# Third layer: averaging the normalised x with the probabilities in two float32r parts, and folded value weights

## What is computed

```python
xn = _layernorm(x, axis=-1)
x = x + _L2_attn_ref(xn, Wq, Wk, Wv) + _L2_ffn_ref(xn, ...)

def _L2_attn_ref(x, Wq, Wk, Wv):           # H, R = 8, 64; d = 128
    Q = (x @ Wq.T).reshape(b, n, H, R)
    K = (x @ Wk.T).reshape(b, n, H, R)
    V = (x @ Wv.T).reshape(b, n, H, d)     # 1024 columns
    attn = softmax(einsum('bnhr,bmhr->bhnm', Q, K), axis=-1)
    return einsum('bhnm,bmhd->bnd', attn, V)      # summed over the heads

def _L2_ffn_ref(x, ...):                   # ternary weights, D_HID = 512
    h = silu(tlin(x, w1)) * tlin(x, w2)
    h = gelu(tlin(h, h1)); h = gelu(tlin(h, h2))
    return tlin(h, w3)
```

## Time and profile before

| | before |
|---|---|
| median of 3 runs (us) | 1756.85 |
| the profiled execution, its time (us) | 1757.49 |
| its span, first to last instruction (us) | 1755.6 |
| mean granted clock of TensorE | 0.975 |
| PE / DVE / ACT / POOL busy (us) | 1668.1 / 996.3 / 837.4 / 406.9 |

### The profile page before, as it was taken

One profiled execution on the slowest core, in us unless ns is written; L12 is line 12 of the kernel. 1 busy time (PEld: TensorE's weight loads), 2 busy tenths in 40 slices (PEclk: granted clock), 3 DMA queues, 4 the chain that ended last, 5 costly groups with the idle time before them and its releaser, 6 DMA issues. The chain is left out here.

```text
span 1755.6 us, 22810 instructions
## 1 busy us (share of the span) xinstructions
PE 1668.1 (95%) x8686; PEld 1004.2 (57%) x8686; DVE 996.3 (57%) x1649; ACT 837.4 (48%) x1048; POOL 406.9 (23%) x331
## 2 busy tenths in 40 slices
PE   7799999999889999999999999999999997999997
PEld 4232222223555667878778786877778673444443
DVE  4555555543675454444555454454555447888886
ACT  5667777776435533333334343343344343444442
POOL 1000000000553322030211112030211205655563
PEclk8799999999889999999999999999999998999999
DMA  2222222222007610000000000000000001000000
GB/s 81 52 49 49 49 49 49 49 49 111 17 26 190 150 27 1 2 0 2 1 1 1 1 1 1 1 1 1 1 1 1 1 1 51 7 7 7 6 13 12
DMA packets 20553, 49.10 MB, mean 28 GB/s; under 512 B 1184, under 2 KB 2080, under 8 KB 19680
## 3 DMA queue, kind: packets, MB, share of 16 engines
q1 hardware_dynamic: 20448, 47.66, 11.1%
HBM read 45.17 MB, written 2.36 MB: 27 GB/s over the span
## 5 line engine op out<-in xcount | busy, mean ns | idle before, releaser
L524 ACT ACTIVATE probs<-ps 128x1024 f32<-128x1024 f32 x256 | 245.9, 1024 | 88.7 <-PE ps L780 85.8
L1972 PEld LDWEIGHTS ps_o<-v,probs 128*128 128x128 f32 x2048 | 236.8, 192 | 35.2 <-issue 30.1
L1972 PE MATMUL ps_o<-v,probs 128*128 128x129 f32 x2048 | 248.2, 278 | 1.7 <-ACT probs L1656 1.2
L1656 ACT ACTIVATE probs<-ps_ring 128x1024 f32<-128x1024 f32 x128 | 127.0, 1023 | 201.9 <-PE ps_ring L1953 201.6
L1748 DVE TENSOR_REDUCE negmax<-ps_o 128x2 f32<-128x1024 f32 x64 | 78.5, 1226 | 137.0 <-PE ps_o L1928 137.0
L794 PE MATMUL ps<-probs,v 128*32 128x512 f32 x1024 | 136.7, 607 | 0.9 <-DVE o_sb L601 0.9
L1649 ACT ACTIVATE xn<-ps_ring,pack 128x512 f32<-128x512 f32 x64 | 40.6, 685 | 164.0 <-PE ps_ring L1493 164.0
L2174 POOL TENSOR_TENSOR rs<-r,state 128x512 f32<-128x512 f32 x64 | 86.2, 1349 | 91.6 <-DVE state L2340 91.6
L1761 DVE RECIPROCAL rden<-ps_o 128x2 f32<-128x2 f32 x128 | 21.5, 168 | 147.8 <-PE ps_o L1972 147.8
L2340 DVE TENSOR_TENSOR_SCAN state<-decay,state,kv 128x511 f32<-128x511 f32 x64 | 99.1, 1548 | 6.9 <-issue 1.5
L780 PEld LDWEIGHTS ps<-q_stack,k_stack 32*128 32x128 f32 x512 | 31.4, 185 | 123.3 <-issue 96.1
(11 more groups left out here) (418 smaller groups left out, 3431.3 us busy)
## 6 DMA issues: line engine op xcount, KB each, us to landing
cwb<-combine_by_expert SPq DMA_DIRECT2D x8, 2048.0 KB
score<-score_by_expert SPq DMA_DIRECT2D x15, 1024.0 KB, 8.0
pack<-pack_dram SPq DMA_DIRECT2D x1, 3840.0 KB, 15.2
x<-x_in SPq DMA_DIRECT2D x2, 1024.0 KB, 6.1
out<-x SPq DMA_DIRECT2D x8, 256.0 KB, 2.0
pack<-pack_dram SPq DMA_DIRECT2D x1, 1992.0 KB, 8.1
pack<-pack_dram SPq DMA_DIRECT2D x1, 1543.0 KB, 6.4
pack<-pack_dram SPq DMA_DIRECT2D x1, 1140.0 KB, 9.4
```

The source lines that it names most:

```text
L524: nc.scalar.activation(probs[n % 3][:, 2 * half:2 * half + 2, :], ps, ACT.Exp, scale=float(HD0) ** -0.5).then_inc(read, 1)
L1656: nc.scalar.activation(probs[:, n % 2, m, :, :], ps, ACT.Exp).then_inc(read, 1)
L1972: last = nc.tensor.matmul(ps_o[:, i, k * (D + 1):(k + 1) * (D + 1)], probs[:, (b * PAIRS + p) % 2, m, j, queries], v[:, m, h, :], start=(m ...
```

## The change

- `values`, `take_v` and `v` go. So does `times_v`.
- `turn_x` turns the normalised x of a batch (four 128x128 transposes); ScalarE and VectorE take it as `xt_high` and `xt_low` [tokens, 128]. Column 0 of it is set to one: since the normalised x sums to zero over the features, feature 0 can be written by the others, and its place carries the ones for the softmax's sum. `fold` is Wv.T with row 0 subtracted from all rows (`fold_first`, once: two float32 matmuls), and a 129th column that picks feature 0.
- `exponent` writes to `exped` (three buffers), then ScalarE makes a second pass, `probs_high`, and GpSimd subtracts to `probs_low`.
- `mix` (b, p, m): 6 float32r matmuls of 512 columns accumulate, over the four key tiles m, the averages of x for both heads in `ps_o`. ScalarE copies them to SBUF (`take_mixed`), and `project_mixed` (4 float32 matmuls of 129 columns for a head) applies `fold`. `normalise` reads that from the ring.
- The low parts of q and k of pairs 2 and 3 are made by GpSimd from a second ScalarE copy, no longer by VectorE.
- `project_mixed` of pair 3 and `turn_attention` run in the next batch; `low_x`, `square`, `rstd`, the mean and variance of the next batch's norm move in the loop.
- Wv moves from the pack of weights that is split in two parts to the pack that is loaded whole; pieces of the split shrink from 480 to 416 columns (L1336, L1352).

```diff
 def ring_order2():
-        for t in range(FT):
-            order += [("gate", b, t), ("qk"[t % 2], b, t // 2), ("v", b, t)]
+        for t in range(FT):
+            order += [("gate", b, t), ("qk"[t % 2], b, t // 2)]
+        order.append(("turn_x", b))
+        if b:
+            order += [("out", b - 1, PAIRS - 1, 0), ("out", b - 1, PAIRS - 1, 1)]
+        order.append(("h1", b, 0))
...
@@ gpsimd
+                for n, name in enumerate("qk"):
+                    was_read(pool, (name, b, 1))
+                    nc.gpsimd.tensor_tensor(single(low[name][:, 2:4, :]), exped[:, n, :, :], high[name][:, 2:4, :], ALU.subtract
+                                            ).then_inc(low_ready, 1)
...
+                for p in range(PAIRS):
+                    for m in range(NBLK):
+                        n = tile_of(b, p, m)
+                        pool.wait_ge(high_ready, b * HIGHS2 + 5 + p * NBLK + m + 1)
+                        nc.gpsimd.tensor_tensor(single(probs_low[:, m, :, :]), exped[:, n % EXPED2, :, :], probs_high[:, m, :, :],
+                                                ALU.subtract).then_inc(low_ready, 1)
+                if b + 1 < B:
+                    low_x(b + 1)
@@ scalar
             def take_high(b, name, i):
...
+                if i:
+                    if b:
+                        act.wait_ge(low_ready, b * LOWS2)
+                    nc.scalar.activation(exped[:, "qk".index(name), :, :], ps, ACT.Copy).then_inc(read, 1)
+            def turned_high(b):
+                ps, _ = filled(act, ("turn_x", b))
+                nc.scalar.activation(single(xt_high[:, :, 1:D]), ..., ACT.Copy).then_inc(high_ready, 1)
+            def take_mixed(b, p):
+                act.wait_ge(values_done, tile_of(b, p, NBLK - 1) + 1)
...
+                nc.scalar.activation(mixed, ps_o[:, :, :], ACT.Copy).then_inc(top_read, 1)
             def exponent(b, p, m):
...
-                nc.scalar.activation(probs[:, n % 2, m, :, :], ps, ACT.Exp).then_inc(read, 1)
+                nc.scalar.activation(exped[:, n % EXPED2, :, :], ps, ACT.Exp).then_inc(read, 1)
+                was_read(act, ("score", b, p, m))
+                if n >= NBLK:
+                    act.wait_ge(values_done, n - NBLK + 1)
+                nc.scalar.activation(single(probs_high[:, m, :, :]), exped[:, n % EXPED2, :, :], ACT.Copy).then_inc(high_ready, 1)
@@ vector
+            def turned_low(b):
+                dve.wait_ge(high_ready, b * HIGHS2 + 5)
+                ps, read = filled(dve, ("turn_x", b))
+                nc.vector.tensor_tensor(single(xt_low[:, :, 1:D]), ..., xt_high[:, :, 1:D], ALU.subtract).then_inc(read, 1)
@@ tensor
+            def mix(b, p, m):
...
+                pe.wait_ge(low_ready, low_count(b, p, m))
+                for n, (lhsT, rhs) in enumerate(((xt_low, probs_high), (xt_high, probs_high), (xt_high, probs_low))):
+                    for j in range(2):
+                        last = nc.tensor.matmul(ps_o[:, j, :], single(lhsT[:, m, :]), single(rhs[:, m, j, :]),
+                                                start=(m == 0 and n == 0), stop=(m == NBLK - 1 and n == 2))
+                last.then_inc(values_done, 1)
+            def project_mixed(b, p, j):
+                ps, done = empty(pe, ("out", b, p, j))
...
+                for m in range(NBLK):
+                    first = (m % 2) * (D + 1)
+                    last = nc.tensor.matmul(ps[:, m // 2, first:first + D + 1], mixed[:, j, m * P:(m + 1) * P], fold[:, 2 * p + j, :],
+                                            start=True, stop=True)
...
                 for p in range(PAIRS):
-                    for s in range(HALVES):
-                        times_v(b, p, s)
...
+                    for m in range(NBLK):
+                        mix(b, p, m)
+                        if p + 1 < PAIRS:
+                            scores(b, p + 1, m)
+                        if p + 2 < PAIRS and m < 2:
+                            maxima(b, p + 2, 2 * m)
+                            maxima(b, p + 2, 2 * m + 1)
+                        if p + 2 < PAIRS and m == 2:
+                            turn_max(b, p + 2)
+                        if p and m in (1, 2):
+                            project_mixed(b, p - 1, m - 1)
```

270 lines of the change are left out of this document (145 added, 125 removed).

## The result

| | before | after |
|---|---|---|
| median of the runs (us) | 1758.09 (4 runs) | 1773.91 (4 runs, 1769.92 to 1776.99) |
| ratio after / before | | 1.0078, 95% interval 1.0057 to 1.0099 |
| the profiled execution, its time and span (us) | 1757.49, 1755.6 | 1771.17, 1769.4 |
| third layer, first gate to the end of the last turned attention (us) | 817.0 | 830.8 |
| of it batch 0 / each of batches 1 to 6 / last batch (us) | 101.7 / 99.7 / 116.9 | 97.3 / 100.8 / 128.8 |

The change makes the kernel slower by 0.8%: 15.8 us between the medians, 13.7 us between the profiled executions. The forecast was 1777. In the profiles the whole difference lies in the third layer (+13.8). A span alone is a coarse measure here: the third layer begins at 633 to 645 us in the profiles of this study, though the code ahead of it is the same apart from the split of the weights.

A forecast was written before the change was run, and what follows sets the result against it. TensorE, busy 95% of the span, was taken as the bound, so its saved work counts less every new wait. Batches 1 to 7 +16.8, batch 0 +1.6, ends +4.0 - 2.4: +20.0 on 1757.49, forecast 1777 us, range 1741 to 1796.

The forecast's parts named there:

- projections, batches 1 to 7: From first gate to `hide1`: walking the chain of hand-offs starts `hide1` at 16.0 instead of 17.24 us, 1.2 us gained.
- feed-forward: Stretch after the projections: the four transposes of the attention, moved here, cost 0.4 us a batch.
- loop, waits: Loop: 1.3 us for the DMA, 0.85 at pair 1's first `project_mixed`, 0.1 for `take_mixed`, less 0.2 before: +2.05.
- loop, TensorE's own work: Loop matmuls: `mix` 22.1, `project_mixed` 5.4, switches 5.0 added; `times_v` 28.6 and its interruptions 2.8 removed: +1.1 us.
- batch 0 in all, with the clock at its start: Batch 0: `hide1` 1.6 us earlier, loop +3.2, and -2.4 from a faster clock at the start; -0.8 in all.
- last batch beyond the others: End of the layer: the tail behind the last `mix` takes 6.4 us instead of 2.5, said +4.0.
- third layer: Whole change: +16.8 us for batches 1 to 7, +1.6 for batch 0, ends +4.0 - 2.4; total +20.0.
- Rival A: Third layer: hand-offs hide and TensorE's own work decides; batch 97.4 us, kernel 1739 us, faster. Chance 0.20.
- B: Projections and loop: the waits (about 38 us in all) are half as long; 1758 us, no change. Chance 0.12.
- C: Projections: idle time drops TensorE's clock in each batch for 12 matmuls, +17 us; 1794 us. Chance 0.08.
- the filled hole: Layer start: `fold_first` fills TensorE's 3.83 us idle time, so 12 matmuls may step 0.23 us: -2.4, or nothing.
- Rival D: Loop: VectorE holds up GpSimd, a tile takes 3.5 us, loop 56 instead of 50.6; 1820 us. Chance 0.04.

The follow-up runs named there:

- e1_table: Changed kernel with ScalarE's table for tanh and GELU loaded ahead of a batch's last `take_mixed` instead of behind it; ratio to before 1.0036, projections 15.02 instead of 15.98 us.
- e8_turn_before: Changed kernel with the maxima of pair 1 turned ahead of the last scores of pair 0 instead of behind them; ratio to before 1.0060, batch 99.9 against 100.8 us.
- e9_split: Changed kernel with the third product of `mix` between scores and maxima in four tiles, four more row-count changes and back a loop; loop 50.64 to 50.70 us against 49.4.
- e5_light: Changed kernel with GpSimd making the low part of only 8 of 512 probability columns in the last batch; last batch 120.8 us against 128.8, one run.
- e6_two_spreads: Changed kernel with two spread buffers for the fourth layer's norm, VectorE centring the next group before scaling the last; ratio to before 1.0032, last batch 119.8 us against 128.8.
- four edits: Changed kernel with earlier table load, `turn_x` before the last k, pair 1's maxima turned earlier, two spread buffers; 1750.79 us, ratio to before 0.9952.
- e10_two_products: Changed kernel without `mix`'s third product (high x times low probabilities); loop 43.1 to 43.2 us in five of the first seven batches against 49.4, one run.

## Why the prediction was right, and where its terms were not

| step | predicted | measured |
|---|---|---|
| projections, batches 1 to 7 | -1.2 (`hide1` at 16.0) | -1.26 (15.98) |
| feed-forward | +0.4 | +0.31 |
| loop, waits | +2.05 | +1.83 (1.94 idle, 0.11 before) |
| loop, TensorE's own work | +1.1 | +0.25 |
| batch 0 in all, with the clock at its start | -0.8 | -4.45 |
| last batch beyond the others | +4.0 | +10.8 |
| third layer | +20.0 | +13.8 |

**What held.** That the loop's work does not fall, and that new hand-offs come on top, was right in sign and nearly in size. The walk of the projections gave each point within 0.1 us: tanh 2.54, the end of the turned low part, `hide1`. The chain was what it said: e1_table took 0.95 out of one link, and 0.96 came back at the end. The DMA's wait was 1.23 where 1.3 was taken, and e8_turn_before showed its cause; ScalarE's second pass took 1.060 (1.058 taken). Rival A (the hand-offs hide) is excluded by the 15.98 and the 1.23; B would have needed waits half as long. C's clock did fall, but not in the projections, where no wait is over 0.65: it fell in the last batch, where no rival had put it.

**The mis-sized term: what the interruptions of `times_v` had cost before.** The loop came out at +2.08 instead of +3.2; 0.85 of the difference is TensorE's own work, 0.2 the waits. The prediction priced the same thing in two ways: 0.42 for each of the 12 changes and back after, from two maxima inside `hide1`, but about 0.3 for each of the 9 interruptions before, 2.8 in all. For those it had counted the longer steps of the 16 records and of the first pair of the scores, and not that of the last pair, 0.32 instead of 0.23. The traces give the same 0.39 to 0.40 on both sides: 9 x 0.39 = 3.5 before, 12 x 0.39 = 4.7 after (5.0 taken). So 0.7 us too little was taken off for before and 0.3 too much added for after; 96 matmuls of `mix` at a step of 0.2325 instead of 0.23 give 0.2 back. That turns +1.1 into +0.3. The rule that the prediction took from the Trainium skill, TensorEngine Tiling (Array Packing), Key Properties, says that changing the tiling mode drains TensorE. The trace agrees in so far as each change costs time in both directions, and e9_split gives the price; but the rule counts against the kernel before, with its 9 interruptions, three quarters as much as against the one after.

**Batch 0 was walked wrongly.** `hide1` was put at 15.2; it started 12.91 after the first gate, with the releaser of gate 3 (`xn` L1799). Without the two `project_mixed` of a batch before, the ring place of `hide1` is that of gate 3: it is three ring uses behind gate 3, not behind `turn_x`, so nothing of the tail is on its path. The clock's part was right: 19.21 before against the 16.8 of the walk is the 2.4 us predicted for the filled hole, and the granted clock at 636 to 640 is 1.00 after.

**The last batch held what no rival had in the right place.** Rival D expected VectorE to hold up GpSimd, tile by tile. It is the other way: in the kernel after GpSimd's subtractions keep to 2.36 to 2.43 us whatever VectorE does, and VectorE's multiplications with two operands in SBUF wait for them, up to 2.8 instead of 0.68 us. The Trainium skill, SBUF — State Buffer, "SBUF: two separate sides", says that an instruction with two SBUF inputs contends with a GpSimd instruction that reads SBUF, and that the one that starts first keeps the ports for its whole length. The traces agree: in the kernel after GpSimd was first each time that a multiplication was longer, and where VectorE was first, in e6_two_spreads, its multiplication took 0.69 and the subtraction 2.57. They also agree in that an instruction with one operand in PSUM is not held up: the turned low part takes 0.69 all eight times (L1776) while GpSimd is at a subtraction. In batches 0 to 6 the one such instruction had slack. In batch 7 there are seven, five of them held up by 1 us or more in a chain that TensorE waits for, and two of these waits were long enough that the clock fell behind them. The tail behind the last `mix` is 4.2 of the +10.8, where 4.0 was predicted, and 6.6 are left for the hold-up. e5_light and e6_two_spreads show cause and remedy; they give back 8.0 and 9.0, more than the 6.6. So without the hold-up, and apart from its tail, the change would cost this batch 1.4 to 2.4 us less than it costs the others; why was not followed.

**The sum.** The errors have opposite signs: 8.0 too much in batches 1 to 6, 3.7 too much in batch 0, 5.5 too little in the last one; 20.0 became 13.8. That the total came within about 3 us of the measured median is in part luck: the parts were further off than their sum.

GpSimd's subtraction was taken as 2.0 by the nearest row of the same form and was 2.39; the range had 2.72, and as said it hid. Why the same form took 2.01 in the second layer is open.

## What to carry over

When a product is made cheaper for TensorE by passes on other engines, price the hand-offs first: here the loop's matmuls saved nothing, and the order decided on either side of zero (+0.8% as written, -0.5% with four edits). When a cost is counted for the new kernel, count it by the same steps in the old one. A table load belongs where its engine idles, not behind the last thing that another engine awaits; a DMA that a wait ends in is cured by issuing it earlier rather than by filling the wait with work that covers something else. And when GpSimd gets a steady stream of work, look through VectorE's program for instructions with both operands in SBUF, in the rare phases too.

## What the runs showed of the hardware

- VectorE, 512 wide, two float32 operands in SBUF: 0.68 us alone, 2.81 us when started 0.15 us behind a 2.4 us subtraction of GpSimd, which was not slowed; when started 0.37 ahead of one (e6_two_spreads) 0.69 us, and the subtraction took 2.57.
- A change between 128-row and 64-row matmuls of 512 columns and back costs 0.39 to 0.40 us, about 0.1 in each of four steps: the last of the old kind and the first of the new one, in both directions.
- Idle times of TensorE of 1.23 us (once a batch) left the granted clock at 1.00. Behind those of 1.67 to 1.71 us at the same place (e9_split and e10_two_products) it fell to 0.50, the 1.2 GHz level, 3 times of 16. In the kernel after it fell behind both of 1.86 and 2.23 us, for the next 6 or so matmuls, which took 0.43 instead of 0.23 us each; in e9_split it fell behind the first of these two only.
- The stretch ahead of the third layer, nearly the same instructions in all kernels, lasted from 633 to 645 us in different executions, at mean granted clocks of 0.95 to 0.93.
